# Attention's division by its sums: from 32-wide transpositions, GpSimd and DMA packs to two transpositions on TensorE

## What is computed

```python
attn = jnp.einsum('bqhd,bkhd->bhqk', q, k) * (1.0 / jnp.sqrt(jnp.float32(D)))
...
attn = jax.nn.softmax(attn + bias[None], axis=-1)
y = jnp.einsum('bhqk,bkhd->bqhd', attn, v).reshape(b, s, e)
return y @ W_proj + b_proj
...
x = x + attn_ref(xn, ...) + ffn_ref(xn, ...)
```

## Time and profile before

| | |
|---|---|
| runs | 561.93 us, median of 3 (561.12 to 563.48) |
| profiled execution | 562.03 us, span 560.3 us |
| TensorE, VectorE, ScalarE, GpSimd busy | 84%, 79%, 61%, 60% of the span |
| mean granted TensorE clock | 0.928 |

### The profile page before, as it was taken

How to read it: one execution, slowest core, us unless ns; L and a number is a source line. 1 busy time by engine, 2 the same in 40 slices (tenths; PEclk the granted TensorE clock), 3 DMA queues, 4 the chain that set the end, 5 groups by cost and what they waited for, 6 DMA issues and landing times.

```text
span 560.3 us, 13084 instructions
## 1 busy us (share of the span) xinstructions
PE 469.0 (84%) x4623; PEld 263.9 (47%) x4623; DVE 440.1 (79%) x870; ACT 343.3 (61%) x656; POOL 337.8 (60%) x569
## 2 busy tenths in 40 slices
PE   1889998667768997997985986799978899999994
PEld 1446564222323442342432342344434589999993
DVE  4987757999999999999999999989724356666663
ACT  3456564136755775776676575578687366666662
POOL 3796751314744556656658456488537347777776
PEclk9999999557987998997999898799998999999999
DMA  8899987822333346443444343358587775655641
GB/s 260 284 234 259 301 283 249 266 77 68 98 95 103 89 122 178 122 141 113 125 136 114 96 124 102 92 172 255 189 262 217 194 145 133 145 139 132 148 103 39
DMA packets 98935, 89.65 MB, mean 160 GB/s; under 512 B 38867, under 2 KB 86995, under 8 KB 98863
## 3 DMA queue, kind: packets, MB, share of 16 engines
q1 hardware_dynamic: 86120, 63.71, 40.3%
q0 software_dynamic: 7360, 18.80, 11.4%
q10 hardware_dynamic: 5392, 6.31, 3.8%
HBM read 42.39 MB, written 37.95 MB: 143 GB/s over the span
## 4 chain that ended last, share of the span: by engine, by line
PE 35%; DVE 33%; POOL 10%; issue 9%; ACT 6%; DMA 5%; SPq 1%; POOLq 0%; DVEq 0%; ACTq 0%
DVE mx L989 15%; PE ps L1252 7%; PE ps L1372 7%; PE ps L1357 4%; PE ps L1387 4%; POOL out_dram L749 3%; DVE mx L984 3%; PE ps L1515 3%; DMA yn<-yn 3%; ACT pr_all L860 2%; PE ps L1505 2%; PE ps L1289 2%; DVE rec_wide L1043 2%; POOL pr_all L743 1%; POOL pr_all L708 1%
## 5 line engine op out<-in xcount | busy, mean ns | idle before, releaser
L860 ACT ACTIVATE pr_all<-ps 128x512 f32<-128x512 f32 x320 | 179.0, 605 | 103.1 <-PE ps L1357 101.6
L989 DVE TENSOR_REDUCE mx<-ps 128x2 f32<-128x768 f32 (+1 forms) x192 | 155.5, 858 | 5.3 <-PE ps L1289 3.8
L1357 PE MATMUL ps<-qs,ks 64*128 64x128 f16 (+3 forms) x512 | 113.9, 320 | 9.1 <-ACT pr_all L860 6.4
L708 POOL TENSOR_SCALAR_AFFINE_SELECT pr_all<-pr_all 128x256 f32<-128x256 f32 (+1 forms) x168 | 69.3, 440 | 50.8 <-ACT pr_all L860 49.8
L1283 PE MATMUL ps<-step,pick 64*128 64x128 bf16 (+1 forms) x640 | 59.0, 224 | 39.2 <-DVE mx L989 22.2
L1372 PE MATMUL ps<-pr_all,vt 128*17 128x512 f32 (+3 forms) x1024 | 88.6, 466 | 1.9 <-ACT ysb L841 1.7
L1289 PE MATMUL ps<-ks,qs 64*128 64x128 f16 (+3 forms) x512 | 81.7, 337 | 0.0
L1357 PEld LDWEIGHTS ps<-qs,ks 64*128 64x128 f16 x512 | 36.1, 98 | 68.7 <-ACT pr_all L860 45.7
L1283 PEld LDWEIGHTS ps<-step,pick 64*128 64x128 bf16 x640 | 28.4, 98 | 72.2 <-DVE mx L989 29.8
L1515 PE MATMUL ps<-vt,pr_all 128*128 x312 | 57.5, 273 | 1.5 <-DVE pr_all L1216 1.5
L1505 PE MATMUL ps<-pr_all,xnp 128*128 128x256 f16 x312 | 55.6, 273 | 0.2 <-DVE pr_all L1211 0.2
(11 more groups left out here) (196 smaller groups left out, 897.0 us busy)
## 6 DMA issues: line engine op xcount, KB each, us to landing
qs<-q_parts SPq DMA_DIRECT2D x64, 100.0 KB
ks<-k_parts SPq DMA_DIRECT2D x64, 96.0 KB
sorted_rows<-ecmp POOLq DMA_DIRECT2D x10, 516.0 KB, 6.7
k_parts<-pr_all SPq DMA_DIRECT2D x16, 256.0 KB, 2.8
q_parts<-pr_all SPq DMA_DIRECT2D x16, 256.0 KB, 2.5
w_h<-in_L_ffn_W_dram SPq DMA_DIRECT2D x16, 256.0 KB, 3.5
w_l<-in_L_ffn_W_dram SPq DMA_DIRECT2D x16, 256.0 KB, 3.0
expert_parts<-w_low SPq DMA_DIRECT2D x32, 128.0 KB, 2.7
```

Source lines behind the costliest of these rows:

```text
L708: pool.affine_select(out=v, in_=v, compare_op=ALU.is_ge, fill=0.0, base=0, pattern=[[0, blocks], [1, P]], channel_multiplier=-1).then_inc( ...
L860: act.activation(dst, src, ACT.Exp, scale=SCORE).then_inc(exp_made, 1)
L989: last = dve.tensor_reduce(mx[:, n1 % 2, :, 2 * g + c, t], ps[:, 2 * (u % 2):2 * (u % 2) + 2, c0:c0 + w], AX, ALU.max)
L1357: last = pe.matmul(dst[:, c0:c0 + w], ks[rows, p, 2 * g + i, t * P:(t + 1) * P], qs[rows, p, 2 * g + i, t * P:S], start=not masked, stop=T ...
```

## The change

Queries go to partitions, so that the division needs no spreading. For each group y, TensorE transposes `ysb` in four 128 x 128 tiles into bank 6 (`turn_y`), VectorE takes the reciprocal of the 128 x 16 sums out of PSUM and multiplies 128 x 256 values into half of `yq` (`scale`). For each pair of groups TensorE transposes `yq` back into bank 6 (`turn_pair`), and ScalarE copies the bank to `yp` (`copy_pair`), which is then packed as before. GpSimd's `normalise`, SyncE's `pack`, `wp_wide` and `last_strip` are gone. A table (`values_at`) sets the slots, counted from the start of group y + 1: first piece of the values 6, the others 8, copy 10, turn 12, scaling 13, and for odd y the turn of the pair 14 and its copy 15. Slots 10 and on lie in group y + 2. From group 27 on other banks (2, 3) are used. ScalarE's work on the experts' weights moves from slot 5 to slot 7. At the end the last pair is turned between the first two experts' matmuls.

```diff
+def values_at():
+    pieces, copies, turns, scales, pairs, packs = ({} for _ in range(6))
+    for y in range(GROUPS - 1):
+        own_, next_ = NSJ * (y + 1), NSJ * (y + 2)
+        first, second, copy, turn, scale, pair, pack = {
+            GROUPS - 3: (4, 6, 8, 10, 10, 12, 13),
+            GROUPS - 2: (3, 5, 7, 9, 9, 0, 0)}.get(y, (6, 8, 10, 12, 13, 14, 15))
...
+        def y_bank(y):
+            return bank[6] if y < AWAY or y == GROUPS - 1 else bank[2]
...
             def copy_y(G):
                 act.wait_ge(y_made, G + 1)
-                after(act, y_normal, G - 1)
+                after(act, y_turned, G - 1)
                 act.activation(ysb[:, G % 2, :], bank[6], ACT.Copy).then_inc(y_copied, 1)
+
+            def copy_pair(m, cols):
+                act.wait_ge(pair_made, m + 1)
+                if m >= HALVES:
+                    act.wait_ge(pj_made, TB * ((m - HALVES) // 2 + 1))
+                act.activation(yp[:, m % HALVES, cols], pair_bank(m)[:, cols], ACT.Copy).then_inc(yp_made, 1)
...
+            def scale(y):
+                dve.wait_ge(y_turned, y + 1)
+                v = y_bank(y).rearrange("p (a b) -> p a b", b=32)
+                mark(dve.reciprocal(rec[:, :], v[:, :, D]))
+                if y % 2 == 0:
+                    after(dve, pair_made, y // 2)
+                heads = v.rearrange("p (t h) b -> p t h b", t=TB)[:, :, :, 0:D]
+                dve.tensor_tensor(yq[:, :, y % 2], heads, rec[:, :].rearrange("p (t h) -> p t h", t=TB)[:, :, :, None]
+                                  .broadcast_to([P, TB, HG, D]), ALU.mult).then_inc(y_scaled, 1)
...
             def with_v(G, blocks):
...
-                        after(pe, y_copied, G)
+                        if G > AWAY:
+                            pe.wait_ge(y_copied, G)
+                        elif G % 2 == 0:
+                            after(pe, yp_made, G // 2)
+                        else:
+                            pe.wait_ge(y_scaled, G)
...
+            def turn_y(y):
+                pe.wait_ge(y_copied, y + 1)
+                after(pe, y_scaled, y)
+                for t in range(TB):
+                    last = pe.transpose(y_bank(y)[:, t * P:(t + 1) * P], ysb[:, y % 2, t * P:(t + 1) * P], idf[:, :])
+                last.then_inc(y_turned, 1)
+
+            def turn_pair(m):
+                pe.wait_ge(y_scaled, 2 * m + 2)
+                after(pe, yp_made, m)
+                for t in range(TB):
+                    last = pe.transpose(pair_bank(m, t >= TB // 2)[:, t * P:(t + 1) * P], yqp[:, 0, t * P:(t + 1) * P], idf[:, :])
+                last.then_inc(pair_made, 1)
...
             with_v(NG * B - 1, range(TB))
-            pe.wait_ge(wide_in, 16 * HG)
-            last_strip(NG * B - 2)
             for t in range(TB):
-                project(B - 1, t, (0,), last_dst(t), begin=False)
+                project(B - 1, t, (0,), last_dst(t), begin=t % 2 == 0)
+            turn_y(GROUPS - 1)
             pe.wait_ge(w1_in, 16 * X)
-            last_strip(NG * B - 1)
             up(0, e[0])
             find_up(1)
+            turn_pair(GROUPS // 2 - 1)
             up(1, e[1])
+            for t in range(TB):
+                project(B - 1, t, (1,), last_dst(t))
```

More of the change, by code:

```diff
@@ L107 @@
 W_ALL = 1280
-PIECES_AT = {3: (0,), 6: (1, 2, 3)}
-PIECES_LAST = {5: (0,), 7: (1, 2, 3)}
+GROUPS = NG * B
+AWAY = GROUPS - 5
+def values_at():
[5 more added lines that the diff above has]
+            GROUPS - 2: (3, 5, 7, 9, 9, 0, 0)}.get(y, (6, 8, 10, 12, 13, 14, 15))
+        pieces[own_ + first], pieces[own_ + second] = (y, (0,)), (y, (1, 2, 3))
+        copies[own_ + copy], turns[own_ + turn], scales[own_ + scale] = y, y, y
+        if y % 2:
+            pairs[own_ + pair], packs[own_ + pack] = y // 2, y // 2
+    return pieces, copies, turns, scales, pairs, packs
+PIECES_AT, COPY_AT, TURN_AT, SCALE_AT, PAIR_AT, PACK_AT = values_at()
 NQ = 4
@@ L313, in score_bank, with pair_bank @@
             return bank[LAST_BANKS[(v - V_LAST) % len(LAST_BANKS)]]
+        def y_bank(y):
+            return bank[6] if y < AWAY or y == GROUPS - 1 else bank[2]
+        def pair_bank(m, late=False):
+            if m == GROUPS // 2 - 1:
+                return bank[6] if late else bank[4]
+            return bank[6] if 2 * m + 1 < AWAY else bank[3]
         def hidden(s):
@@ L418, in shift_rows @@
                     shift_half(sp, n, e)
-            def pack(G):
-                half, r0 = G // 2, HALF * (G % 2)
-                sp.wait_ge(y_normal, G + 1)
-                if half >= HALVES:
-                    sp.wait_ge(pj_made, TB * ((half - HALVES) // 2 + 1))
-                for j in range(HG):
-                    sp.dma_start(yp[r0 + D * j:r0 + D * (j + 1), half % HALVES, :], yn[32 * j:32 * j + D, G % 2, :]
-                                 ).then_inc(yp_in[G % NG], 16)
             def store_sum(n):
@@ L470, in _ @@
                         load_group(n + 2, g)
-                    if NG * n + g >= 2 and g != 2 and (n, g) != (B - 1, NG - 1):
-                        pack(NG * n + g - 2)
                     if (n, g) >= (ROUTED + 2, 0):
@@ L1192, in _ @@
                             make_shift(n + 1)
[L1193 to L1194 removed]
+                        if SLOTS_ROW * n + u in SCALE_AT:
+                            scale(SCALE_AT[SLOTS_ROW * n + u])
                         sums = RESIDUAL if n < B - 1 else RESIDUAL_LAST
@@ L1456, in _ @@
                             count_marks(2)
-                        pieces = PIECES_AT if n < B - 1 else PIECES_LAST
-                        if k in pieces and G >= 1:
-                            with_v(G - 1, pieces[k])
+                        v = NSJ * G + k
+                        if v in PIECES_AT:
+                            with_v(*PIECES_AT[v])
+                        if v in TURN_AT:
+                            turn_y(TURN_AT[v])
+                        if v in PAIR_AT:
+                            turn_pair(PAIR_AT[v])
                         places = PROJECT if n < B - 1 else PROJECT_LAST
@@ L1522, in last_dst @@
                 return bank[7 - 2 * (t // 2)][:, t % 2 * E:(t % 2 + 1) * E]
-            def last_strip(G):
-                pe.wait_ge(y_normal, G + 1)
-                for t in range(TB):
-                    last = pe.matmul(last_dst(t), yn[:, G % 2, t * P:(t + 1) * P], wp_wide[:, G % 2, :],
-                                     start=(G < NG * B - 1 and t % 2 == 0), stop=(G == NG * B - 1), skip_group_check=True)
-                    if G == NG * B - 1:
-                        last.then_inc(pj_made, 1)
             pe.wait_ge(exp_made, NSJ * NG * B)
```

78 lines of the change are left out of this document (22 added, 56 removed).

## The result

The changed kernel takes **629.65 us** (median of 4 runs, 627.84 to 632.71) beside 561.52 for the kernel before: ratio 1.122, 95% interval 1.1185 to 1.1248. That is +68 us; the forecast was +27, its range ended at 606.

A forecast was written before the change was run, and what follows sets the result against it. VectorE's list was taken to bound images 0 to 5. Image terms +1, +12, +9 and +3.7 sum to +25.9; with +0.7 for the tail, 562.0 becomes 588.6, so 589 us; own range 575 to 606, 8 in 10 within 558 to 606.

The forecast's parts named there:

- Three of the signs I had named: Checks named in advance: image 3's fourth group 13 to 14 us, its second no longer, first gather 10.5 to 11.5 us after.
- I take 0.14 each: TensorE's added transpositions: 0.14 us each, 0.55 for four; 0.11 or 0.2 would move the forecast by -5 or +9.
- the 12 forecast: Images 1 to 3: image 3 grows by 4.0 us, images 1 and 2 alike, +12 together.
- as laid out: Image 3's odd groups priced step by step: second group 11.4 us (-0.8), fourth 13.45 us (+3.3).
- 9.6 each: Image 3's first and third groups, priced in the same way: 9.6 us each, +1.3 and +0.3.
- a projection of both halves: TensorE's projection in each group laid out: priced at 0.86 us.
- I leave that where it is: Tail: the first expert's sorted rows still land at 444.1 us; the tail as a whole counts +0.7 us.
- only its odd groups lose: Image 6: only the odd groups grow, by 2.3 and 1.4 us, +3.7 together.
- So for six images the time is VectorE's list.: Attention, images 0 to 5: VectorE, 95% busy, sets the time, and what hides behind it is free.
- VectorE's saving wins: Rival: TensorE's lead keeps VectorE fed in attention, 26 us come off, 537 us, or 550 with half lost; chance 0.16.
- Dear transpositions: Rival: TensorE's transpositions take 0.35 us each, 33 us more over 13 pairs, 622 us; chance 0.03.
- Forced holes alone: Rival: only VectorE's forced idle time per pair counts, 36 us against 26 saved, say 568 us; chance 0.17.

The follow-up runs named there:

- the fill version: The changed kernel with six unused 512-column matmuls on TensorE in the wait ahead of each pair's turn, all waits kept: 615.5 us, 1.096.
- the version without waits: The changed kernel with the scaling moved from slot 13 to 12 and the pair's turn from 14 to 15: 576.4 us, 1.0245.
- the spread version: The changed kernel with its division at slots 6, 7, 8, 10, 10, 12, 13, same instructions: 580.5 us, 1.035 beside 560.6.
- before_fill: The kernel before with eight unused 512-column matmuls in the second group of each image: 1.004.

## Why the prediction was wrong

**Right: the mechanism, and the order of its waits.** Turning the pair waits for a scaling that stands behind a reduction, the unit behind it comes late, and the values wait for the pair's copy. A turn of four takes 0.66 us in the timeline for the 0.55 assumed, the scaling with its step 0.70 for 0.73, the wait 1.6 for 1.7. TensorE's wait for the scaling comes to 22.8 us in 12 waits, 1.9 each. VectorE's busy time fell by 33 (25), its idle time rose to 88 (50). Three of the signs I had named stood against it: image 3's fourth group is 14.8 us (13 to 14), its second, which was not to be longer than its 12.24, is 13.56, and the first gather comes 9.7 us behind the first expert's first matmul at 509.84 (10.5 to 11.5). No run shows the 0.14 us for a transposition, nor the 0.2 in the forecast's range: both were estimates of mine. The traces have 0.66 us for the four of a turn at a clock of 1.00, 0.165 for each of them, and 0.86 for the turn of the pair at 308.21, at a mean clock of 0.68.

**The step that failed: every price at one clock.** "I take 0.14 each, 0.55 us for four, near the lower end, since that row is of the same clock": the forecast held the clock of attention for given, for the transpositions and for all work around them. The change makes TensorE stand still for 1.6 us and then hands it 3 us of dense work, and that work ran at 0.54. With the waits left in and the clock at 0.99 (the fill version), images 1 to 3 grow by 13.9 us against the 12 forecast; without the fill, by 25.4. So for them the missing term is the clock, which the sum had at nothing: 11 us here, 16 in the whole. In image 3 of the fill version the two odd groups take 11.1 and 13.2 us, as laid out (11.4 and 13.45). Its first and third take 11.2 and 11.0 where 9.6 each was forecast. In the third it is neither the clock nor a forced wait: at a clock of 1.00 TensorE alone is busy 10.15 us there (8.60 before), and the version without waits still needs 10.5. So 9.6 us was less than TensorE's own work. One price in it was too low at the higher level too: a projection of both halves, 0.86 us by the last strips, takes 1.06 at a clock of 1.00, here and in the kernel before.

**The second, and by size the larger: images 0, 4 to 6 and 7 were not laid out.** The forecast missed by 41 us, and 16 of them are the clock; the other 25 are mostly here. Only image 3 was laid out; the others were scaled from it. The last image was left out of the sum ("I leave that where it is"), and the changed kernel takes 5.8 us longer from the 27th copy to the last. Even in the fill version images 4 and 5 grow by 13.7 (forecast 9), image 6 by 8.7 (3.7), image 0 by 7.8 (1). For image 6 I had said that only its odd groups lose. There VectorE has few maxima to make, and TensorE is the fullest engine in the kernel before too. Windows of the kernel before and of the version with both waits removed, from the 24th copy to the 28th:

```profile
380.26:414.65 34.39, 30.65 (x363) 14.11 (x361) 24.14 (x39) 26.95 (x53) 23.73 (x29) 1.00 0.70 215
```

```profile
387.72:427.62 39.90, 34.63 (x384) 17.22 (x383) 16.83 (x28) 27.60 (x53) 22.07 (x26) 1.00 0.57 188
```

4.0 us more of TensorE's time, 5.5 us more in length, both at a clock of 1.00, with hardly a wait for the scaling. That fits a stretch in which TensorE's work shows in full, but no run tests it by itself. The 15 us that this version still loses, against the kernel before of the same set, are image 6 (3.6), the time behind the 27th copy (5.6), image 0 and what lies ahead of it (4.6), and 1.8 in images 1 to 5 together. For the last image and the tail, 7 us in the changed kernel and 0.7 forecast, and for image 0 nothing was tried by itself.

**"So for six images the time is VectorE's list."** This was the first reading of the profile, and it didn't hold: 28 us of that list taken away gave back about 9, and none in images 1 and 2. It did no harm to the laid-out groups, but it made the rival "VectorE's saving wins" look like one in six. In the version without waits, where it was to win, VectorE's time fell by 32 us and the kernel was 15 slower.

**The rivals.** Dear transpositions came nearest in time (622) for the wrong reason: a turn of four took 0.66 us and not 1.4, and 160 transpositions cost the kernel before 5.5 us. Forced holes alone (568) had no clock either. The range ended at 606 because every bound in it was a bound on a price, none on the state in which the work runs.

**Open.** How the 53 us that two moves give back divide between waits and clock: the fill version's 16 is a clock's worth with the waits left in, and fills don't reach every low stretch. And which engine binds the spread version: it can't take VectorE's old work back (48 us), while the same TensorE work is mostly hidden in the old order. Several chains of about equal length, with one unit's lead between the engines, would do both; no run separates them. Nor did a run take out the low stretches of the kernel before.

## What to carry to other kernels

In this kernel a short wait ahead of dense work on TensorE was paid for twice, as a wait (1.61 us in the group laid out) and by the lower clock behind it (0.54 over 3.3 us); so in a stretch that TensorE nearly fills, look at how long it stands still, not only at its sum, and try each new instruction one place later or its producer one place earlier before judging an idea. Here two places made 53 us of 68.

A busy share of 95% says that an engine has little room for more, not that the time falls with its work: take the work away, add nothing, and see who ends its waits then (here 28 us less of VectorE's work gave back 9). Lay out one group of every kind, not one group for all, and hold each laid-out group's length against the busy time of every engine in it.

## What the runs showed that I had not expected

- Useless matmuls made the kernel faster by 16 us: the mean granted clock in attention went from 0.88 to 0.93 with 78 of them put into waits. In the kernel before a filler put elsewhere left the clock at 0.93 and the time the same (1.004).
- A stretch of 3 us in which TensorE worked 1.4 and waited 1.6 was followed by 3.3 us at a mean granted clock of 0.54.
- On other chips the same kernel before took 613 to 620 us (medians). By the trace of before_fill images 0 to 3 of attention are as long there as here, and the difference lies behind them.
